# Head outputs from quarter-array pieces, smaller value maps and exchanged PSUM banks in a gated cross-attention and mixture-of-experts block

## The reference, cut to what matters

```python
# x: (4, 1024, 256) f32, context: (4, 154, 192) f32; 8 heads of 64
q = (layernorm(x) @ W_q), k = (context @ W_k), v = (context @ W_v)     # split into 8 heads of 64
sim = einsum('bihd,bjhd->bhij', q, k) * 64 ** -0.5, masked by mask
attn = softmax(sim)                                                      # over 154 keys
out = einsum('bhij,bjhd->bihd', attn, v).reshape(b, n, 512)              # "head outputs"
x = x + tanh(g_xattn) * (out @ W_o + b_o)
# then a router (6 of 32 experts in 8 groups), routed experts and a shared expert, added with tanh(g_ffn)
```

## Time and profile before

| | us |
|---|---|
| time, median of 3 runs | 738.55 (737.33 to 740.41) |
| span of the profiled execution, from its first to its last instruction | 736.5 |
| TensorE busy | 692.0 |
| VectorE busy | 523.0 |
| GpSimd busy | 471.8 |
| ScalarE busy | 454.0 |

### The profile page before, as it was taken

How to read it: one execution, slowest core, us unless ns; L and a number is a source line. 1 busy time by engine, 2 the same in 40 slices (tenths; PEclk the granted TensorE clock), 3 DMA queues, 4 the chain that set the end, 5 groups by cost and what they waited for, 6 DMA issues and landing times.

```text
span 736.5 us, 17797 instructions
## 1 busy us (share of the span) xinstructions
PE 692.0 (94%) x5400; PEld 593.4 (81%) x5400; DVE 523.0 (71%) x1785; ACT 454.0 (62%) x1299; POOL 471.8 (64%) x478
## 2 busy tenths in 40 slices
PE   8978898999999999989999899999999999999887
PEld 7867797888888888876665799999899888898755
DVE  1667568787878787786473466666568888888884
ACT  1267576778797969693523765556776576565531
POOL 1344442466565656667777767777777777777773
PEclk9999999999999999999999999999999999999999
DMA  8980000135222222253838986666679999999855
GB/s 285 380 279 1 1 3 1 54 95 201 87 97 91 94 94 86 102 193 108 321 124 267 325 286 189 217 194 189 196 239 337 344 341 362 340 376 324 273 194 170
DMA packets 86303, 144.73 MB, mean 197 GB/s; under 512 B 14647, under 2 KB 60994, under 8 KB 85185
## 3 DMA queue, kind: packets, MB, share of 16 engines
q1 hardware_dynamic: 52560, 68.09, 29.6%
q0 software_dynamic: 19968, 52.34, 19.1%
q10 hardware_dynamic: 13680, 23.17, 9.4%
HBM read 78.00 MB, written 69.73 MB: 201 GB/s over the span
## 4 chain that ended last, share of the span: by engine, by line
PE 62%; DVE 17%; ACT 6%; DVEq 5%; issue 5%; POOL 3%; DMA 1%; ACTq 0%; POOLq 0%; SPq 0%
PE ps L1513 11%; PE ps L1528 10%; PE ps L1499 5%; PE ps L1373 5%; PE ps L1308 5%; PE ps L1318 5%; ACT att L602 4%; PE ps L1262 3%; PE ps L1407 3%; POOL token_parts L556 3%; PE ps L1208 2%; PE ps L1295 2%; PE ps L1229 2%; PE ps L1385 2%; PE ps L1395 2%
## 5 line engine op out<-in xcount | busy, mean ns | idle before, releaser
L463 POOL DMA_INDIRECT routed_rows<-x_n,slots x120 | 119.9, 999 | 68.0 <-issue 32.0
L556 POOL DMA_INDIRECT token_parts<-hid,place x112 | 116.2, 1038 | 39.1 <-issue 26.5
L1513 PEld LDWEIGHTS ps<-att 128*128 128x128 f32 x768 | 99.3, 192 | 19.7 <-issue 8.8
L700 ACT ACTIVATE att<-ps 128x512 f32<-128x512 f32 x96 | 57.3, 597 | 88.6 <-PE ps L1499 82.1
L1513 PE MATMUL ps<-att 128*128 128x128 f32 x768 | 102.6, 277 | 6.1 <-DVE att L1121 3.3
L602 ACT ACTIVATE att<-ps,nmax,rstd 128x154 f32<-128x154 f32 x176 | 81.9, 494 | 14.7 <-DVE nmax L836 14.6
L1308 PE MATMUL ps<-att,big 128*64 128x128 f32 x1024 | 70.1, 279 | 15.9 <-ACT att L619 11.3
L713 ACT ACTIVATE att<-big 128x256 f32 x224 | 80.2, 408 | 2.4 <-issue 2.1
L1528 PE MATMUL ps<-big,att 128*128 x300 | 78.3, 384 | 2.9 <-DVE picked L1130 2.9
L1308 PEld LDWEIGHTS ps<-att,big 128*64 128x64 f32 x1024 | 59.4, 137 | 23.5 <-ACT att L619 13.8
L619 ACT ACTIVATE att<-ps 128x512 f32<-128x512 f32 (+1 forms) x96 | 48.4, 552 | 32.3 <-PE ps L1295 32.3
(11 more groups left out here) (265 smaller groups left out, 1557.4 us busy)
## 6 DMA issues: line engine op xcount, KB each, us to landing
mid<-routed_rows SPq DMA_DIRECT2D x168, 138.0 KB
big<-token_parts ACTq DMA_DIRECT2D x57, 256.0 KB
routing<-routed_rows SPq DMA_DIRECT2D x56, 138.0 KB
x_n<-token_parts ACTq DMA_DIRECT2D x27, 256.0 KB
routed_rows<-pad_row SPq DMA_DIRECT2D x1, 4416.0 KB
routed_rows<-pad_row SPq DMA_DIRECT2D x32, 138.0 KB
x_all<-in_x SPq DMA_DIRECT2D x4, 1024.0 KB, 12.5
big<-in_x_t SPq DMA_DIRECT2D x4, 1024.0 KB, 14.3
```

The source lines that it names most:

```text
L463: nc.gpsimd.indirect_dma_start(rows, bass.IndirectOffsetOnAxis(ap=slots[:, t, k:k + 1], axis=0), normed(t), None).then_inc(s_sca[t // TB % ...
L556: nc.gpsimd.indirect_dma_start(parts, bass.IndirectOffsetOnAxis(ap=place[:, p // 2 % 8, p % 2 * 2 + j:p % 2 * 2 + j + 1], axis=0), y_sb[p ...
L700: A.activation(xt(p), ps[:, p % 2, :], ACT.Copy).then_inc(s_xts, 1)
L1513: ins = M(ps[:, 2 + p % 2, j * P:(j + 1) * P], w_up[p % 2][:, j, c * P:(c + 1) * P], xt(p)[:, j * 256 + c * P:j * 256 + (c + 1) * P], star ...
```

## The change

Three things are changed.

1. Head outputs. The heads are now in two banks, the first four (q = 0) in columns 256 to 511 of bank 7, the last four (q = 1) in the same columns of bank 6. Parts of a head that cover at most 64 rows of a chunk are products of 64 rows by 64 columns, a quarter of the array; there are 16 of these and 4 of 128 rows by 64 columns. The quarters come in two stretches, one ahead of the four full ones and one behind. In each stretch one row half of the array works for bank 7 and the other for bank 6; between them TensorE waits for its own first stretch (`s_turn`). The order of the transposed chunks is changed (`CHUNKS`), so that the three copied groups hold chunks 1, 2, 3, 6, then 7, 8, 0, 4, then 5, 9.
2. Value maps. 768 columns for each batch instead of 1024: an even group of 512 columns with 4 full products and 8 of half the columns, and an odd group of 256 columns with 8 of half the columns. The zero padding around the context is narrower (`WIN`).
3. Banks. Queries, the query weights' mean and the second half of the normalised transposes go to bank 4, the second group of transposed probabilities to bank 6. The output projection takes its four parts in the order 2, 3, 0, 1, as the two banks are saved bank 6 first.

The core of the diff (memory offsets, bank numbers in copies and the narrower clearing are left out):

```diff
-HEAD_ORDER = ((0, 0), (1, 1), (0, 1), (1, 2), (2, 2), (3, 3), (2, 3), (3, 4), (4, 5), (5, 6), (4, 6), (5, 7), (6, 7),
-              (7, 8), (6, 8), (7, 9))
+HEADS_BANK = (7, 6)
+CHUNKS = (1, 2, 3, 6, 7, 8, 0, 4, 5, 9)
+FULL_KEYS = ((0, 0, 0), (3, 4, P))
+LOWER_KEYS = ((0, 1, INNER), (1, 1, INNER + P), (2, 3, 2 * P), (1, 2, 3 * P))
+UPPER_KEYS = ((2, 2, 2 * P), (1, 1, 3 * P), (2, 3, INNER), (3, 3, INNER + P))
...
             def save_heads(T):
                 act.wait_ge(s_hq, T + 5)
-                A.activation(att_t, ps[:, 7, :], ACT.Copy).then_inc(s_at, 1)
+                A.activation(att_t.rearrange("p (a n) -> p a n", a=2), ps[:, HEADS_BANK[1]:HEADS_BANK[0] + 1, D:2 * D],
+                             ACT.Copy).then_inc(s_at, 1)
...
+            def map_half(b, bank, half, h, key, at, c):
+                return M(ps[half * DH:(half + 1) * DH, bank, at:at + P], ctx_w[:, c, b, KEY_0 + key:KEY_0 + key + DH], two_heads(h, c),
+                         start=c == 0, stop=c == 1, skip_group_check=True)
+
+            def values_map(b, bank):
+                for h, key, at in ((0, 0, 0), (3, KEY_0, P)):
+                    for c in range(2):
+                        M(ps[:, bank, at:at + P], ctx_w[:, c, b, KEY_0 + key:KEY_0 + key + P], two_heads(h, c), start=c == 0,
+                          stop=c == 1, skip_group_check=True)
+                for h, low, high, at in ((2, DH, 0, 2 * P), (1, KEY_0 + DH, KEY_0, 3 * P)):
+                    for c in range(2):
+                        map_half(b, bank, 0, h, low, at, c)
+                        ins = map_half(b, bank, 1, h, high, at, c)
+                return ins
+
+            def ends_map(b, bank):
+                for h, key, at in ((0, P, 0), (1, -KEY_0, P)):
+                    for c in range(2):
+                        map_half(b, bank, 0, h, key, at, c)
+                        ins = map_half(b, bank, 1, h + 2, key, at, c)
                 return ins
...
-                    for w in range(4 * n, 4 * n + 4):
-                        h, ch = w // 2, (w + 1) // 2
-                        win = P + ch * P - h * JP
-                        for c in range(2):
-                            ins = M(ps[:, bank, w % 4 * P:(w % 4 + 1) * P], ctx_w[:, c, b, win:win + P],
-                                    wv[:, c, :].rearrange("p (g n) -> p g n", g=2)[:, :, h * DH:(h + 1) * DH],
-                                    start=c == 0, stop=c == 1, skip_group_check=True)
+                    ins = (ends_map if n else values_map)(b, bank)
...
-                for c in range(4 * g, min(4 * g + 4, NCH)):
-                    ins = nc.tensor.transpose(ps[:, (3, 4, 3)[g], c % 4 * P:(c % 4 + 1) * P],
+                for i in range(4 * g, min(4 * g + 4, NCH)):
+                    c = CHUNKS[i]
+                    ins = nc.tensor.transpose(ps[:, (3, 6, 3)[g], i % 4 * P:(i % 4 + 1) * P],
...
+            def head_piece(T, q, rows, piece, start, stop=False):
+                h, c, at = piece
+                n, at = CHUNKS.index(5 * q + c) * P, at + q * DH
+                return M(ps[h % 2 * DH:(h % 2 + 1) * DH, HEADS_BANK[q], D + h // 2 * P:D + (h // 2 + 1) * P],
+                         v_all[T // (NT // NB)][rows, at:at + DH], prob_t[rows, n:n + P], start=start, stop=stop, skip_group_check=True)
+
             def heads_out(T):
-                b = T // (NT // NB)
+                every, lower, upper = slice(0, P), slice(0, DH), slice(DH, P)
                 if T >= 1:
                     pe.wait_ge(s_x1, T)
-                for i, (h, c) in enumerate(HEAD_ORDER):
-                    if i in (0, 7, 13):
-                        pe.wait_ge(s_pt, 3 * T + (0, 7, 13).index(i) + 1)
-                    at = (h % 4 + c % 5) * P + h // 4 * DH
-                    ins = M(ps[h % 2 * DH:(h % 2 + 1) * DH, 7, h // 2 * P:(h // 2 + 1) * P], v_all[b][:, at:at + DH],
-                            prob_t[:, c * P:(c + 1) * P], start=c * P <= h * JP, stop=(c + 1) * P >= h * JP + J,
-                            skip_group_check=True)
+                pe.wait_ge(s_pt, 3 * T + 1)
+                head_piece(T, 0, lower, LOWER_KEYS[0], True)
+                head_piece(T, 0, lower, LOWER_KEYS[1], True)
+                pe.wait_ge(s_pt, 3 * T + 2)
+                head_piece(T, 1, upper, UPPER_KEYS[0], True)
+                head_piece(T, 1, upper, UPPER_KEYS[1], True)
+                for i in (2, 3):
+                    head_piece(T, 0, lower, LOWER_KEYS[i], False)
+                    ins = head_piece(T, 1, upper, UPPER_KEYS[i], False)
+                ins.then_inc(s_turn, 1)
+                for i in range(2):
+                    head_piece(T, 0, every, FULL_KEYS[i], False)
+                pe.wait_ge(s_pt, 3 * T + 3)
+                for i in range(2):
+                    head_piece(T, 1, every, FULL_KEYS[i], False)
+                pe.wait_ge(s_turn, T + 1)
+                for i in range(4):
+                    head_piece(T, 1, lower, LOWER_KEYS[i], False, True)
+                    ins = head_piece(T, 0, upper, UPPER_KEYS[i], False, True)
                 ins.then_inc(s_hq, 1)
```

More of the change, by code:

```diff
@@ L39 @@
 DUMMY = NE * REGION
-WIN = P + J + P
-V_SIZE = N_WIN * P
+KEY_0, V_SIZE = 32, INNER + 2 * P
+WIN = KEY_0 + P + DH
 V_AT = NT * D
@@ L239, in flamingo_block @@
         s_hq = sem("queries_and_heads_out_psum")
+        s_turn = sem("heads_first_half_rows")
         s_q = sem("queries")
@@ L307, in x2t_bank @@
         def x2t_bank(b, j):
-            return 5 if j == 0 else 6 if b < NBLK - 1 else 4
+            return 5 if j == 0 else 4
         def down_bank(t):
@@ L346, in load_ctx @@
                 for c in range(2):
-                    sp.dma_start(ctx_w[:, c, b:b + 2, P:P + J],
+                    sp.dma_start(ctx_w[:, c, b:b + 2, KEY_0:KEY_0 + J],
                                  ctx_t[:, c, b * J:(b + 2) * J].rearrange("p (b j) -> p b j", b=2)).then_inc(s_ctx[b // 2], 16)
@@ L432, in _ @@
             for c in range(2):
-                nc.gpsimd.memset(ctx_w[:, c, :, 0:P], 0.0)
-                nc.gpsimd.memset(ctx_w[:, c, :, P + J:WIN], 0.0)
+                nc.gpsimd.memset(ctx_w[:, c, :, 0:KEY_0], 0.0)
+                nc.gpsimd.memset(ctx_w[:, c, :, KEY_0 + J:WIN], 0.0)
             for r in range(3):
@@ L592, in _ @@
                 else:
-                    A.activation(v_all[b][:, 512 * n:512 * n + 512], ps[:, bank, :], ACT.Copy).then_inc(s_ma, 1)
+                    w = 2 * P if n else INNER
+                    A.activation(v_all[b][:, INNER * n:INNER * n + w], ps[:, bank, 0:w], ACT.Copy).then_inc(s_ma, 1)
             def exps(T, q):
@@ L810, in _ @@
                 else:
-                    V.tensor_copy(v_all[b][:, 512 * n:512 * n + 512], ps[:, bank, :]).then_inc(s_mv, 1)
+                    w = 2 * P if n else INNER
+                    V.tensor_copy(v_all[b][:, INNER * n:INNER * n + w], ps[:, bank, 0:w]).then_inc(s_mv, 1)
                 if g == 5:
@@ L820, in _ @@
                     for c in range(KC):
-                        ins = V.tensor_tensor(wq[:, c, :], wq[:, c, :], ps[:, 6, :], ALU.subtract)
+                        ins = V.tensor_tensor(wq[:, c, :], wq[:, c, :], ps[:, 4, :], ALU.subtract)
                     ins.then_inc(s_wc, 1)
@@ L1195, in _ @@
             for i in range(WARM):
-                M(ps[:, 6, 0:P], ones_bf[:], ones_bf[:], start=True, stop=True)
+                M(ps[:, 4, 0:P], ones_bf[:], ones_bf[:], start=True, stop=True)
             pe.wait_ge(s_clr, 1)
@@ L1219, in _ @@
                     for c in range(2):
-                        ins = M(ps[:, bank, 0:2 * J], wk[:, c, n * P:(n + 1) * P], ctx_w[:, c, 2 * b:2 * b + 2, P:P + J],
+                        ins = M(ps[:, bank, 0:2 * J], wk[:, c, n * P:(n + 1) * P], ctx_w[:, c, 2 * b:2 * b + 2, KEY_0:KEY_0 + J],
                                 start=c == 0, stop=c == 1)
@@ L1235, in _ @@
                     for c in range(KC):
-                        ins = M(ps[:, 6, :], mean_w, wq[:, c, :], start=c == 0, stop=c == KC - 1)
+                        ins = M(ps[:, 4, :], mean_w, wq[:, c, :], start=c == 0, stop=c == KC - 1)
                     ins.then_inc(s_wm, 1)
@@ L1317, in attn_out @@
                 for m in range(MC):
-                    ins = M(ps[:, 7, 0:D], att_t[:, m * P:(m + 1) * P], wo[:, m, :], start=m == 0, stop=m == MC - 1,
+                    ins = M(ps[:, 7, 0:D], att_t[:, (m + 2) % MC * P:((m + 2) % MC + 1) * P], wo[:, m, :], start=m == 0, stop=m == MC - 1,
                             skip_group_check=True)
@@ L1323, in normed_2_t @@
                 pe.wait_ge(s_xn2, TB * b + 2 * j + 2)
-                if j == 1 and b < NBLK - 1:
+                if j == 1:
                     pe.wait_ge(s_q, min(TB * b + 9, NT))
-                elif j == 1:
-                    pe.wait_ge(s_pt, 3 * NT)
                 elif b >= 1:
@@ L1379, in down @@
                 if i == 0:
-                    pe.wait_ge((s_q, s_x1)[h], NT)
+                    pe.wait_ge((s_at, s_x1)[h], NT)
```

12 lines of the change are left out of this document (7 added, 5 removed).

## The result

The changed kernel ("after" in what follows, as the other is "before") takes 750.5 us (median of four runs, 749.19 to 751.2) where the kernel before, measured beside it, takes 739.48: a ratio of 1.0151, 95% interval 1.0131 to 1.017, so 11 us slower. The forecast was 740.9 with a range up to 747.5: **the prediction was wrong**, outside its range, on the side that was given 0.30. The profiled execution's own time is 750.89.

What follows compares the result with a forecast made beforehand. TensorE, busy 94% of the span and holding 62% of the last-ending chain, was taken as what time gained or lost reaches the end through. Attention +4.9 and value maps -2.6 gave +2.3 on 738.55: 740.9 us, range 735.0 to 747.5.

Steps and rivals of the forecast that it cites:

- the side that was given 0.30: Whole kernel: the outcome measurably slower than before, given a chance of 0.30, against 0.60 for same and 0.10 for faster.
- The wait that moves: Head outputs with a late second copy: all three stretches, 1.74 us, remain behind it instead of 1.24, +0.50 us each.
- Head outputs that TensorE runs through: Attention tiles without a wait inside: three stretches of 0.58, 1.74 us against 1.90, a gain of 0.16 us each.
- rival 3: Head outputs: quarters run only two abreast, 2.64 us each, +19.4 us in all, 758.0 us; chance 0.08.
- rival 1: Head outputs: the two inner shape changes cost nothing, 1.50 us for 1.74, -2.3 us in all, 736.2 us; chance 0.20.
- Behind the wait: Waiting head outputs: a sign, 4 instructions ahead of the second-copy wait and 36 behind, 1.74 us from the copy's end.
- The count of tiles: Attention: 7 chain tiles at -0.16, 7 and 5 at +0.50, 13 at nothing, +4.9 us; four-tile period grows 0.34.
- rival 2: Attention: the late second copy bounds all tiles, +8.8 us, 747.4 us; sign, four-tile period over 1 us longer; chance 0.15.
- Value maps: Kernel's start: one batch takes 2.92 us instead of 3.57, four batches -2.6 us, all on TensorE's chain.
- without a break: First 60 us: the chain of waits is TensorE alone from 12.14 on.
- Rival 4: Attention: the second copy is early everywhere, all 19 chain tiles gain 0.16, -5.6 us, 732.9 us; chance 0.05.
- Banks at nothing: Queries moved to bank 4, second group's transposes to bank 6, heads copied from two banks: priced at no cost.

Runs made afterwards that it cites:

- e1: The kernel before with only its wait for the second copy moved from ahead of product 7 to ahead of product 2: 748.05 us, ratio 1.0103.
- e2: The changed kernel with 24 idle products ahead of the first piece in seven of the head outputs: 742.95 us, ratio 1.0042.
- e5: The kernel before with its second-copy wait ahead of product 2 and 24 idle products in the same seven tiles as e2: 743.94 us, ratio 1.0051.
- e3: The changed kernel with ScalarE's second and third copies placed behind the first three exponentials instead of all eight: 742.02 us, ratio 1.0019.
- e4: The kernel before with only the banks of queries and transposes exchanged: 739.83 us, ratio 0.9997.
- e6: The changed kernel with e3's early copies and idle products behind the first two iterations' queries and ahead of head outputs 1 and 3: 736.42 us, ratio 0.9955.
- e8: The changed kernel with e2's idle products plus others behind the first two iterations' queries and ahead of head outputs 1 and 3: 741.14 us, ratio 1.0019.
- e9: The kernel before with e3's early copies and e6's early-tile idle products, without the change: 737.77 us, ratio 0.9972.

## Why the prediction was wrong

**The step that failed is "The wait that moves".** It priced one thing, the work that remains behind a late copy (+0.50 us), and took the standing ahead of it as free: TensorE idle "should grow" stood among the signs, without a price. The term that lacked is the clock. TensorE stood 1.36 us in the earlier trace rows and ran on at full clock; with ten instructions taken out from ahead of the wait it stands longer, and in four tiles, behind standings of 1.62, 1.94, 1.90 and 2.11 us, half the clock is granted for 3.41 us, at 0.99 to 1.62 us each, +5.8 in all. Not every such standing brings it: behind 1.62 to 1.67 us at 55.07, 164.27, 242.15 and 280.14 the clock stayed full. e1 shows that the moved wait brings it, e2 and e5 that it goes when TensorE stands less. In the two traces the 12.6 us are 5.0 of work behind late copies (as e2 has it), 5.8 of clock, 1.8 less by the earlier start, and 3.6 from the expert loop to the end. The Trainium skill (TensorE: Matmul & The Clock Gate, Why this matters for your kernels) advises against idle gaps between bursts of products because throughput drops after them, but the gaps it names are longer than these. The traces show the drop behind 1.62 to 2.11 us too, and the measurement decides.

The other steps, one by one:
- **Head outputs that TensorE runs through**: 1.74 us predicted, 222.62 to 224.41 = 1.79 measured, 0.60 a stretch instead of 0.58. Quarters do run four abreast, and rival 3 (2.64) is gone; the changes of shape do cost, and rival 1 (1.50) is gone too. The gain is 0.11, not 0.16.
- **Behind the wait**: 4 instructions ahead and 36 behind, as predicted, and 191.92 to 193.69 = 1.77 from the copy on for 1.74.
- **The count of tiles**: the period that the prediction named, 37.96 us, is 39.89 after (182.73 to 222.62), 1.93 longer, which by its own sign would be rival 2; but 1.62 of that is the stretch at 204 us. In e2, with full clock there, the five periods from 103.87 to 295.18 are 0.26, 0.61, 0.40, 0.30 and 0.36 us longer than before, where 0.34 was predicted. Rival 2, over 1 us, is gone. From the first scores to the expert loop e2 loses 5.03 us for a predicted 4.9.
- **Value maps**: 2.92 us a batch predicted, 2.79 measured, so -3.1 for four and not -2.6. But keys and queries that follow a change of shape pay for it: 2.27 at 18.43 where keys took 2.08, 1.98 at 27.27 where the earlier trace rows have 1.79. From the maps' start to the first mask row it is 34.03 - 12.65 = 21.38 us for 35.87 - 12.14 = 23.73: **-2.35** for -2.6. The keys ahead of them started 0.51 us later in this execution (8.27 for 7.76; the 56 opening products took 5.66 us for 4.88), for which no cause was looked for, so the scores came 1.84 earlier instead of 2.6. The prediction's "without a break" holds up to 37.38 us, where the chain goes to VectorE; the maps lie ahead of that.
- **Rival 4**, the second copy early everywhere: not so, it is waited for in 24 places; e3 had to make it so.
- **Banks at nothing**: right (e4).

The last stage adds what no step named. The chains of after and before at their ends, and then the granted clock of after:

```profile
734.12 4.26 DMA token_parts<-big,place
738.46 4.46 DMA big<-token_parts
742.96 3.54 PE ps L1600 x8
```

```profile
724.21 3.37 DMA token_parts<-big,place
...
727.66 4.17 DMA big<-token_parts
...
731.87 2.01 PE ps L1558 x8
```

```profile
742.00:749.00 7.00, 3.52 (x8) 2.33 (x8) 1.27 (x3) 0.00 (x0) 0.00 (x0) 0.76 0.11 39
```

The last write to DRAM starts 9.91 us later than before, takes 0.89 more to the read behind it, the read 0.29 more, and the last products, ahead of which TensorE stood 3.79 us for the read (0.96 before), take 3.54 us for 2.01, at a lowered clock (0.76 over the last 7 us). 9.91 + 0.89 + 0.29 + 1.53 = 12.62, the difference of the two spans. This end varies among the traces: the write took from 2.9 (e1) to 4.7 us (e6), and the last eight products 2.01 in e1, e2, e4, e5, e8 and e9 but 2.81 in e6 and 3.69 in e3. That the spans differ by 12.6 and the medians by 11.0 is mostly the choice of executions: the profiled one of before is taken at 738.55, 0.93 under the median that after is compared with, and that of after took 750.89, 0.39 over its own.

## What to carry to other kernels

A wait moved forward on a busy engine has two prices: the work that now queues behind it, and the standing itself, which grows by the work that no longer lies ahead of it (1.36 us before, 1.94 after). On TensorE read the granted clock of the microseconds after every longer standing of the kernel before, and ask of each standing that will grow what a half-clock stretch there would add. If one appears, move the producer ahead rather than the wait, or fill the standing with idle products: here 24 of them in each of seven tiles turned 750.5 us into 742.95, the early copies by themselves 742.02, and the early copies with idle products in the first tiles 736.42, where the same kind of filling brought the kernel before 2.2 us.

## What the runs showed of the hardware beyond that

- In a loop in which TensorE is busy for 93% of the time, standings of 1.94 and 2.01 us were followed by 3.41 us at the lower clock. The granted clock was still full for some time after TensorE had started again (0.99 from 202.50 to 204.00; 0.2 to 1.6 us in the eight stretches behind late copies after and in e1), so the loss shows in other instructions than those that waited. Of the standings of 1.62 to 1.81 us in these two traces two of ten were followed by such a stretch, of those of 1.90 to 2.25 us all six; what decides among the shorter ones no run here shows.
- Runs of one kernel seem to differ in this: e1's six go from 745.54 us at a mean granted clock of 0.993 to 751.43 at 0.984. They spread over 5.9 us, the kernel before beside them over 4.0 in 27 runs.
- Four quarters of the array work abreast in f32: 20 products, 16 of them on quarters, in 1.79 us, while 16 half-column products take 1.90. The changes of shape, 0.11 to 0.19 us each, take up most of what the finer cut saves.
